# Splitting the keys' and queries' products of layers 1 to 3 into float32r halves, and five scatters ahead of the attention's root

## The reference, cut to what matters

```python
for i in range(DEPTH):                                   # DEPTH = 4
    h = _layernorm(x, ln1_g[i], ln1_b[i])
    x = x + _linear_attn(h, Wq[i], Wk[i], Wv[i], Wo[i], bo[i])
    h = _layernorm(x, ln2_g[i], ln2_b[i])
    x = x + (gelu(h @ W1[i] + b1[i]) @ W2[i] + b2[i])
# in _linear_attn, 8 heads of 32
q = softmax(split(x @ Wq) * scale, axis=-1)
k = softmax(split(x @ Wk) * scale, axis=-2)              # over the nodes
context = einsum('bhnd,bhne->bhde', k, v)
# in the GNN block
sums = segment_sum(edge_attr, src, num_segments=n)
```

## Time and profile before

| what | value |
| --- | --- |
| median of 3 runs | 2965.56 us (2961.09 to 2966.38) |
| the profiled execution, its own time | 2963.2 us |
| its span in the trace | 2961.5 us |
| PE busy | 2678.0 us, 90% of the span |
| PEld busy | 2464.6 us, 83% |
| DVE busy | 2092.0 us, 71% |
| POOL busy, without the time to issue a DMA | 1753.0 us, 59% |
| ACT busy | 1545.6 us, 52% |
| chain that ended last | PE 36%, POOL 30%, DVE 15%, issue 14% |

### The profile page before, as it was taken

How to read it: one execution, slowest core, us unless ns; L and a number is a source line. 1 busy time by engine, 2 the same in 40 slices (tenths; PEclk the granted TensorE clock), 3 DMA queues, 4 the chain that set the end, 5 groups by cost and what they waited for, 6 DMA issues and landing times.

```text
span 2961.5 us, 56289 instructions
## 1 busy us (share of the span) xinstructions
PE 2678.0 (90%) x18946; PEld 2464.6 (83%) x18946; DVE 2092.0 (71%) x4764; ACT 1545.6 (52%) x3001; POOL 1753.0 (59%) x1613
## 2 busy tenths in 40 slices
PE   4888999999999999998999999989999998995298
PEld 2677899999988999997889999879999898995265
DVE  8887666767666676676567666688888887896055
ACT  0655466666535556653565655444444445763065
POOL 2011287777768888886888887055555554222566
PEclk7999999999999999999999999989999998997599
DMA  5001323222232322224222332143333332210243
GB/s 124 28 29 35 90 57 69 62 61 65 58 98 67 65 63 66 62 56 110 63 61 62 66 69 48 37 122 93 88 88 87 89 83 62 61 37 24 81 121 100
DMA packets 255561, 207.89 MB, mean 70 GB/s; under 512 B 165505, under 2 KB 194386, under 8 KB 255277
## 3 DMA queue, kind: packets, MB, share of 16 engines
q1 hardware_dynamic: 197678, 162.55, 20.8%
q0 software_dynamic: 57600, 41.75, 7.2%
HBM read 136.93 MB, written 70.16 MB: 70 GB/s over the span
## 4 chain that ended last, share of the span: by engine, by line
PE 36%; POOL 30%; DVE 15%; issue 14%; DMA 2%; ACT 1%; DVEq 1%; ACTq 0%; SPq 0%; POOLq 0%
PE bank L380 32%; POOL edges_sorted L735 23%; POOL r L713 3%; DVE hidh_lo L1311 3%; PE bank L1815 2%; POOL tokens_sorted L800 2%; DVE xh L1275 2%; DVE staging L1181 1%; DVE oh L1499 1%; PE bank L2268 1%; POOL ehl L752 1%; DMA staging<-in_edge_attr 1%; DVEq L1478 1%; DVE bn L1266 1%; DVE kmask L1175 1%
## 5 line engine op out<-in xcount | busy, mean ns | idle before, releaser
L735 POOL DMA_INDIRECT edges_sorted<-staging,pos_i x850 | 1061.6, 1249 | 252.0 <-issue 236.8
L851 ACT ACTIVATE hid<-bank,b1p 128x250 f32<-128x250 f32 x800 | 331.3, 465 | 350.0 <-PE bank L380 307.0
L1311 DVE TENSOR_TENSOR hidh_lo<-hid,hidh_hi 128x500 fp32r<-128x500 f32 x400 | 321.3, 804 | 251.5 <-ACT hidh_hi L857 181.2
L380 PE MATMUL bank<-w_hi,hidh_hi 128*125 128x256 f32 x1600 | 471.5, 295 | 23.8 <-DVE hidh_lo L1311 23.8
L380 PE MATMUL bank<-h_hi,w_hi 128*128 128x250 f32 x1600 | 479.3, 300 | 10.5 <-DVE h_lo L1295 10.4
L380 PE MATMUL bank<-w_hi,hidh_lo 128*125 128x256 f32 x1600 | 453.4, 283 | 0.0
L380 PE MATMUL bank<-w_lo,hidh_hi 128*125 128x256 f32 x1600 | 451.4, 282 | 0.0
L380 PE MATMUL bank<-h_hi,w_lo 128*128 128x250 f32 x1600 | 448.3, 280 | 0.0
L380 PE MATMUL bank<-h_lo,w_hi 128*128 128x250 f32 x1600 | 445.0, 278 | 0.0
L380 PE MATMUL bank<-wqk,h 128*125 128x256 f32 x1600 | 370.3, 385 | 0.6 <-ACT mbc L902 0.6
L380 PEld LDWEIGHTS bank<-wqk,h 128*125 128x125 f32 x1600 | 298.3, 190 | 43.9 <-ACT h L819 1.1
(11 more groups left out here) (284 smaller groups left out, 5787.1 us busy)
## 6 DMA issues: line engine op xcount, KB each, us to landing
staging<-edges_sorted SPq DMA_DIRECT2D x103, 260.0 KB
staging<-in_edge_attr SPq DMA_DIRECT2D x50, 531.2 KB
queries<-qn SPq DMA_DIRECT2D x100, 250.0 KB
qin<-queries SPq DMA_DIRECT2D x100, 250.0 KB
edges_sorted<-staging,pos_i POOLq DMA_INDIRECT x850
rows_in<-edges_sorted SPq DMA_DIRECT2D x50, 260.0 KB
yin<-tokens_sorted SPq DMA_DIRECT2D x81, 127.0 KB
raw<-in_L_mix_W SPq DMA_DIRECT2D x8, 1024.0 KB, 5.4
```

The costliest lines, as they stand in the source:

```text
L380: return nc.tensor.matmul(o, left, right, start=start, stop=stop, skip_group_check=True)
L735: nc.gpsimd.indirect_dma_start(out=edges_sorted, out_offset=bass.IndirectOffsetOnAxis(ap=pos_i[:, i:i + 1], axis=0), in_=stage[:, slot, j, ...
L851: a = nc.scalar.activation(hid[c % 2][:, j, :], chunks(PH[c % 2])[:, j, :], ACT.Gelu, bias=b1p[:, 2 * c + j:2 * c + j + 1])
L1311: nc.vector.tensor_tensor(hidh[c % 2][1][:, :, :], hid[c % 2][:, :, :], f32(hidh[c % 2][0][:, :, :]), ALU.subtract).then_inc(f_lo, 1)
```

## The change

From layer 1 on, keys and queries are made as three float32r products of halves. For this each layer's weights are split once, in step t = 1: `mix_high` casts `wqk` to `wqk_hi` on ACT at the start of the step, behind a wait for all five DMAs of `w_mix`, and `mix_low` makes `wqk_lo` on DVE. Each group's `h2` is cast to `h2_hi` at the end of `key_affine`, and `key_low` makes `h2_lo` on DVE, which lies in the place of `h2` itself. `keys` waits for `k_lo` in place of `k_h` and `w_mix`. Layer 0 keeps the plain products. `wqk_hi`, `wqk_lo` and `h2_hi` lie where the masks of the edge ranks lay, so the first `mix_high` also waits for `e_acc`. The counts of `k_h` change with the additional steps; a semaphore, `rw_T`, is merged into `gcol_pe`.

In `SCATTERS_STEP`, layer 0 goes from (6, 5) to (5, 6), layer 1 from (6, 6) to (5, 6), layer 2 from (6, 6) to (5, 7). Counted out, 253 scatters stand in layer 0 before and after, 300 and then 275 in layer 1, 269 and then 294 in layer 2, and 28 in the two drains between them.

```diff
-SCATTERS_STEP = {0: (6, 5), 1: (6, 6), 2: (6, 6), 3: (4, 4)}
+SCATTERS_STEP = {0: (5, 6), 1: (5, 6), 2: (5, 7), 3: (4, 4)}
...
+        h2_lo = sb("h2_lo", [128, KC, GT], F32R, layers)
...
+        wqk_hi = sb("wqk_hi", [128, KC, 2 * D], F32R, halves_place)
+        wqk_lo = sb("wqk_lo", [128, KC, 2 * D], F32R, halves_place)
+        h2_hi = sb("h2_hi", [128, KC, GT], F32R, halves_place)
...
                 a.then_inc(k_h, 1)
+                if l:
+                    act.wait_ge(k_h, input_ready(l, g))
+                    nc.scalar.copy(h2_hi[:, :, :], h2[:, :, :]).then_inc(k_h, 1)
+
+            def mix_high(l):
+                if l == 1:
+                    act.wait_ge(e_acc, 2 * KINDS)
+                act.wait_ge(w_mix, 80 * (l + 1))
+                nc.scalar.copy(wqk_hi[:, :, :], wqk[:, :, :]).then_inc(k_h, 1)
...
+                if later and t == 1:
+                    mix_high(l + 1)
                 if 1 <= t < LAST:
                     copy_queries(l, t + 1)
...
+            def mix_low(l):
+                dve.wait_ge(k_h, high_weights(l))
+                nc.vector.tensor_tensor(wqk_lo[:, :, :], wqk[:, :, :], f32(wqk_hi[:, :, :]), ALU.subtract).then_inc(k_lo, 1)
+
+            def key_low(l, g):
+                dve.wait_ge(k_h, input_high(l, g))
+                nc.vector.tensor_tensor(h2_lo[:, :, :], h2[:, :, :], f32(h2_hi[:, :, :]), ALU.subtract).then_inc(k_lo, 1)
...
                 if later and t in MAX_AT:
                     block_max(l + 1, MAX_AT[t])
+                if later and t == 1:
+                    mix_low(l + 1)
+                if later and t >= 1:
+                    key_low(l + 1, t - 1)
...
+            def mixed(o, l, part):
+
+                inputs, weights = (h2_hi, h2_lo), (wqk_hi, wqk_lo)
+                for j in range(PAIR):
+                    rows = slice(j * P, (j + 1) * P)
+                    for k in range(KC):
+                        if l == 0:
+                            a = mm(o[0:P, j * D:(j + 1) * D], h2[:, k, rows], wqk[:, k, part], k == 0, k == KC - 1)
+                        else:
+                            a = mm3(o[0:P, j * D:(j + 1) * D], at(inputs, slice(None), k, rows), at(weights, slice(None), k, part),
+                                    k == 0, k == KC - 1)
...
             def keys(l, g):
                 m = nth(l, g)
-                pe.wait_ge(k_h, m + 1)
-                pe.wait_ge(w_mix, 80 * (l + 1))
+                if l:
+                    pe.wait_ge(k_lo, input_low(l, g))
+                else:
+                    pe.wait_ge(k_h, input_ready(l, g))
+                    pe.wait_ge(w_mix, 80)
```

More of the change, by code:

```diff
@@ L173, in build @@
         kst = sb("kst", [P, TILES, 2], F32, layers)
-        h2 = sb("h2", [128, KC, GT], F32, layers)
+        input_place = ExitStack()
+        h2 = sb("h2", [128, KC, GT], F32, input_place)
+        input_place.close()
+        h2_lo = sb("h2_lo", [128, KC, GT], F32R, layers)
         qd = sb("qd", [P, PAIR, D], F32, layers)
@@ L1067, in _ @@
             nc.scalar.copy(g2[0][:, :, :], raw_g2[:, :, :]).then_inc(gw_hi, 1)
-            act.wait_ge(rw_T, 1)
+            act.wait_ge(gcol_pe, 2)
             nc.scalar.copy(rwT[:, :, :], chunks(PQ, KC, EXP)).then_inc(rw_ready, 1)
@@ L1612, in drain @@
                 subtract_max(L, first + 1)
+                if l >= 0:
+                    key_low(L, LAST)
                 key_sum(L, first)
@@ L1926, in keys @@
                     pe.wait_ge(m_copied, maxima)
-                for j in range(PAIR):
-                    for k in range(KC):
-                        a = mm(PK[0:P, j * D:(j + 1) * D], h2[:, k, j * P:(j + 1) * P], wqk[:, k, 0:D], k == 0, k == KC - 1)
-                a.then_inc(k_prod, 1)
+                mixed(PK, l, slice(0, D)).then_inc(k_prod, 1)
             def queries_of(l, g):
@@ L1937, in queries_of @@
                     pe.wait_ge(s_sub, m)
-                for j in range(PAIR):
-                    for k in range(KC):
-                        a = mm(PMQ[0:P, j * D:(j + 1) * D], h2[:, k, j * P:(j + 1) * P], wqk[:, k, D:2 * D], k == 0, k == KC - 1)
-                a.then_inc(s_prod, 1)
+                mixed(PMQ, l, slice(D, 2 * D)).then_inc(s_prod, 1)
             def idle_products(count):
```

25 lines of the change are left out of this document (20 added, 5 removed).

## The result

| what | before | after |
| --- | --- | --- |
| median | 2965.97 us (4 runs, 2961.09 to 2973.09) | 2933.86 us (4 runs, 2933.07 to 2934.28) |
| span of the profiled execution | 2961.5 us | 2931.4 us |
| PE busy | 2678.0 us | 2633.3 us |
| DVE busy | 2092.0 us | 2140.1 us |
| ACT busy | 1545.6 us | 1577.9 us |

The changed kernel takes 0.989 of the time of the kernel before, with a 95% interval of 0.9871 to 0.991: 32 us less. The forecast was 2938 us (2923 to 2955), from a sum of 26 less.

The account below looks back on a forecast made before the run. The prediction took PE to bound layer 0 and POOL layers 1 and 2. Its terms, -9 + 2 + 4.6 - 22 - 1.5 - 0.5, summed to -26.4 us, giving a forecast of 2938 us, range 2923 to 2955.

Parts of the forecast that it names:

- The bound by stage: Layers 0 to 2: layer 0 goes at PE's pace, layers 1 and 2 at POOL's with twelve scatters a step.
- The products: Keys and queries on PE: 24 products of halves take 2.82 us in place of 3.45, saving 0.63 us per group.
- The rival with loads that are not hidden: Keys and queries on PE: 24 products take the 3.45 us of before; 2960 us in all, chance 0.04.
- Layer 0, steps 8 to 24: PE has no slack there, so 0.63 us per step comes off in about 15 steps: -9 us.
- The halves of the inputs: New cast on ACT and subtraction on DVE cost nothing in a step; the drains together +2 us, 0 to +4.
- The weights' wait: mix_high on ACT in layer 0 waits for the weights: PE waits 3.6 us, then lower clock; +4.6 us net.
- Layer 1: One scatter fewer a step: 455.3 us in place of 477.4, -22; its end at POOL another -1.5.
- Layer 2: Twelve scatters stay, so 20.24 us per step stays whatever PE gains: -0.5 us, from -3 to +2.
- The root's place: Attention's root on POOL stands behind five scatters: gives or takes nothing in a full round, counted at 0.
- interlock: Rival: PE's and POOL's near paces interlock; layer 1 gains 11 in place of 23.5, layer 0 6; 2953 us, chance 0.13.
- The weights were not early: Rival: weights land early and layer 2 sheds 3 more; neither +4.6 nor the drains' +2 counts; 2928 us, chance 0.11.

Follow-up runs that it names:

- even_table: Changed kernel with eleven scatters in every step of layer 2, the 19 left over in steps with a block's maximum and layer 2's step 0; ratio 0.9837.
- cast_late: Changed kernel with the cast of the weights' high half moved between the second and third gelu of step 1; ratio 0.9864 to the kernel before.
- low_late: Changed kernel with key_low moved behind the fourth hidden_low of the step; ratio 0.9999 to the kernel before.
- the repetition: The changed kernel itself, unedited, run and profiled once more; ratio 0.9889 to the kernel before.
- products_alone: Changed kernel with the scatter table of the kernel before; 2979.8 us where the kernel before took 2980.69, ratio 0.9996.
- table_alone: Kernel before with the new scatter table and plain products everywhere; ratio 0.99 to the kernel before.
- root_behind_six: Changed kernel with as many scatters per layer, but six instead of five ahead of the attention's root; ratio 0.9933 to the kernel before.
- two_products_tiny_low: Changed kernel without the low-input, high-weights product, and the subtraction for the keys' input cut to two elements per partition; ratio 0.9802 to the kernel before.
- eleven_late: Changed kernel with the weights' cast behind the second gelu, eleven scatters in every step of layers 0 to 2, 20 per drain; 2901.14 us against 2951.22, ratio 0.9833.
- nineteen_late: As eleven_late, but with 19 scatters in a drain in place of 20; ratio 0.9811 to the kernel before.

## Why the forecast held, point by point

- **The bound by stage.** Right. The two halves of the change alone and `even_table` show it: layer 1 was POOL's and became PE's, layer 2 stayed POOL's, and eleven scatters make it PE's as well.
- **The products.** Right: 2.85 us in place of 3.45, 2.82 forecast. The rival with loads that are not hidden is out. A rule of the Trainium skill (TensorE: Matmul & The Clock Gate, part 3, "What overlaps and what doesn't") has a weight load run beside a matmul only for other row groups; the trace does not agree, since 24 loads over the whole array left a pitch of 0.119 us.
- **Layer 0, steps 8 to 24.** -9 forecast; the last fifteen steps gave -6.7 and -9.1. But the seven ahead of them gave another -3 to -4 (-3.2 in `cast_late`, where no wait stands ahead of them): the first of these (17.7 to 17.8 us, now 16.9 to 17.3) were at PE's pace too. The forecast has no term for them and no reason why.
- **The halves of the inputs.** Right: PE waits for them in no step of layers 0 to 2, only for 1.0 us or less in a drain. In most steps the low half is 1.1 to 1.5 us early. `low_late` shows what that cover was worth. The ways between layers changed by -0.6 and +2.1 (+1.3 and +0.9 in the repetition), some +2 as forecast, behind layers 0 and 2.
- **The weights' wait.** Right in place and cause: 3.66 us measured, 3.6 forecast, with the 3.4 us of half clock behind it. That the size fits to 0.1 us is partly luck, since it was 2.82 in the repetition, 3.49 in `products_alone` and 5.1 in `even_table`; the cast began 5.9 and 6.4 us after the last load was issued, where the forecast borrowed 5.4 from a larger load. The sum had 4.6 for the wait and the clock together, less the first group's saving. PE was 5.3 and 6.3 us later at the `attend` of the next step, of which 0.4 and 2.1 lie ahead of the cast, so 5.0 and 4.2 are this term: its size was right.
- **Layer 1.** -22 forecast, -23.6 and -24.8 measured. Its end was -1.5 in the forecast and -4.0 and -5.4 in the traces, and `table_alone` has -3.9 of it. This term was mis-sized: it counted one scatter less ahead of the last root, but POOL had been further behind than one. The way to layer 2 was 69.9 us before; the way to layer 1, where the layer ahead goes at PE's pace, was 65.3.
- **Layer 2.** -0.5 forecast, +1.5 and -0.6 measured. That PE's saving is worth nothing there was right.
- **The root's place.** Counted at 0. `root_behind_six` is 4 and 10 us longer, but `products_alone` bears out only 2 of the 5 us of its layer 2, so the runs suggest a small gain and don't show its size.
- **The rivals.** No interlock: in the last fifteen steps of layer 1 a step is 19.6 us, PE's pace, though the paces are only 0.1 to 0.6 apart. The forecast's distance of 0.7 was too large because it took POOL's scatters to stay as they were: in the last fifteen steps of layer 1 their mean was 1239 ns before and 1276 in the changed kernel. The weights were not early.

The sum, -26.4, was 3 to 9 us short of the -30 and -35 in the layers. The mechanisms held; what it lacked are the steps 1 to 7 of layer 0 (-3 to -4), the end of layer 1 (-2.5 and -4) and another -2 to -3 within layer 1. Against that, in the first of the two executions the last fifteen steps of layer 0 and layer 2 came out 4 worse than their terms, and in the second the clock at the start of layer 0 cost 2. That the total came so close owes something to errors of opposite sign.

## What to carry to other kernels

Where two engines run at nearly the same pace, try an edit to each of them together: either alone may be worth nothing and be thrown away, as the products were here with the old table (0.9996), though they are worth 25 to 30 us with an even one. Look at each stage for which engine has no idle time left, and level the movable work until the same engine is the bound in all of them. And a wait for a load belongs behind the work that does not need it: one place in ACT's order was worth 4 to 5 us in layer 0, one place in DVE's the whole gain by the ratio.

## What the runs showed of the hardware

The time in which POOL issues a scatter depends on what else the kernel does. Nothing of the scatter was edited, but in layer 0 its mean went from 1248 ns before to 1277 in the changed kernel and 1268 in the repetition (231 scatters each, from the third copy of the queries to the last), with medians of 1.18 to 1.19 us: a few take up to 1.7. This fits the loss in layers 1 and 2 with the products alone: in layer 1 the mean went from 1240 to 1255 ns, which over 266 scatters makes 4.0 us, and the layer got 4 longer; in layer 2 it went from 1246 to 1257, 2.8 us over 258, and the layer got 2 longer. The Trainium skill (GPSIMD Engine Reference, section 1) says that the interfaces of POOL to the core's memory are shared with VectorE, with contention when a VectorE instruction has two inputs from that memory, among others; the new subtractions have two. `two_products_tiny_low` (1256 to 1240) goes that way. But `low_late` does the same subtractions and has a mean of 1242 in layer 0, so the amount of such work is not all of it; how the two engines' work falls together in a step must count as well.

The staging load of 531 KB, issued at the start of a layer beside its other loads (`eleven_late` and `nineteen_late`), was used 14.8 us and 15.7 us after its issue. Where it is needed first decides where it has to be issued.
